# Top-k cross attention: the row maximum goes into the mask on GpSimd, and the guard's transpose, copy and transfer go

## The reference

```
q = (h @ w_q + b_q).reshape(B, L, H, D)
kv = (ctx @ w_kv + b_kv).reshape(B, Lc, 2, H, D)
k, v = (kv[:, :, 0], kv[:, :, 1])
scores = jnp.einsum('bqhd,bkhd->bhqk', q, k) / jnp.sqrt(jnp.float32(D))
top_s, top_i = jax.lax.top_k(scores, TOPK)          # TOPK = 16
attn = jax.nn.softmax(top_s, axis=-1)
vg = jnp.take_along_axis(v_bh[:, :, None, :, :], top_i[..., None], axis=3)
o = jnp.einsum('bhqk,bhqkd->bqhd', attn, vg).reshape(B, L, C)
```

## Time and profile before

| | before |
| --- | --- |
| median of 3 runs | 1315.63 us |
| span of the profiled execution | 1318.7 us |
| TensorE busy | 1221.3 us, 93% |
| VectorE busy | 1162.2 us, 88% |
| ScalarE busy | 994.5 us, 75% |
| GpSimd busy | 849.7 us, 64% |
| mean granted TensorE clock | 0.963 of full |

### The profile page before, as it was taken

How to read it: one execution, slowest core, us unless ns; L and a number is a source line. 1 busy time by engine, 2 the same in 40 slices (tenths; PEclk the granted TensorE clock), 3 DMA queues, 4 the chain that set the end, 5 groups by cost and what they waited for, 6 DMA issues and landing times. The chain is left out here.

```text
span 1318.7 us, 38821 instructions
## 1 busy us (share of the span) xinstructions
PE 1221.3 (93%) x13667; PEld 860.3 (65%) x13667; DVE 1162.2 (88%) x3854; ACT 994.5 (75%) x2001; POOL 849.7 (64%) x1134
## 2 busy tenths in 40 slices
PE   6888798999999999999999999999999999989897
PEld 5665476667676766666676766676676766656564
DVE  4469899999999999998999999999999999897443
ACT  3644487879797978878797979888797878776754
POOL 1314397958686886859496877959595868666310
PEclk8768799999999999999999999999999999989999
DMA  6531111202111121202121121312030211110110
GB/s 202 139 94 32 36 39 40 66 22 69 39 50 50 29 79 34 65 19 71 30 58 43 42 66 26 82 28 66 17 85 23 74 26 34 34 26 17 34 34 17
DMA packets 111390, 67.23 MB, mean 51 GB/s; under 512 B 13837, under 2 KB 107871, under 8 KB 111199
## 3 DMA queue, kind: packets, MB, share of 16 engines
q1 hardware_dynamic: 109166, 63.71, 18.2%
q10 hardware_dynamic: 2032, 1.05, 0.3%
HBM read 22.33 MB, written 4.19 MB: 20 GB/s over the span
## 5 line engine op out<-in xcount | busy, mean ns | idle before, releaser
L1762 ACT ACTIVATE prob<-turned_score 128x1024 f32<-128x1024 f32 x320 | 325.9, 1018 | 115.5 <-PE turned_score L1434 107.4
L2021 POOL TENSOR_TENSOR pair<-full,pair 128x512 f16<-128x512 f32 x182 | 210.6, 1163 | 108.5 <-ACT pair L1727 100.3
L2027 POOL TENSOR_SCALAR far<-far 128x512 bf16<-128x512 bf16 x256 | 158.0, 617 | 110.9 <-DVE far L1937 92.3
L1923 DVE MATCH_REPLACE8 rest<-top,score 128x256 f32<-128x256 f32 x512 | 207.7, 413 | 0.0
L1937 DVE MATCH_REPLACE8 far<-best,rest 128x256 bf16<-128x256 f32 x512 | 205.3, 408 | 1.0 <-issue 1.0
L1920 DVE MAX8 top<-score 128x8 f32<-128x256 f32 x512 | 192.2, 416 | 6.8 <-PE score L1434 6.4
L1910 DVE TENSOR_REDUCE rowmax_l<-score 128x4 f32<-128x1024 f32 x121 | 147.3, 1217 | 42.0 <-PE score L1434 29.4
L1434 PE MATMUL work<-pair_n,w_m_hi 128*128 128x256 f16 x1024 | 173.5, 274 | 1.4 <-ACT pair_n L1727 1.3
L1434 PE MATMUL work<-pair_n,w_m_lo 128*128 128x256 f16 x512 | 139.8, 273 | 0.0
L1727 ACT ACTIVATE pair<-full 128x512 f16<-128x512 f32 x192 | 121.0, 630 | 18.7 <-DMA q_stack_l<-pair 1.0
L1434 PEld LDWEIGHTS work<-pair_n,w_m_hi 128*128 128x128 f16 x1024 | 96.1, 98 | 22.3 <-issue 9.9
(11 more groups left out here) (206 smaller groups left out, 3190.9 us busy)
## 6 DMA issues: line engine op xcount, KB each, us to landing
k_stack_t<-pair SPq DMA_DIRECT2D x96, 64.0 KB, 2.3
k_stack_l<-pair SPq DMA_DIRECT2D x96, 64.0 KB, 2.3
k_stack_w<-pair SPq DMA_DIRECT2D x93, 64.0 KB, 2.3
q_stack_w<-pair SPq DMA_DIRECT2D x93, 64.0 KB, 2.3
q_stack_t<-pair SPq DMA_DIRECT2D x93, 64.0 KB, 2.3
q_stack_l<-pair SPq DMA_DIRECT2D x93, 64.0 KB, 2.3
ctx_t<-in_ctx_turned SPq DMA_DIRECT2D x16, 256.0 KB, 2.8
ctx_l<-in_ctx SPq DMA_DIRECT2D x16, 256.0 KB, 2.9
```

The costliest lines, as they stand in the source:

```text
L1762: act.activation(prob[:, at:at + 2, :], both_b[:, :, :], ACT.Exp).then_inc(exp_done, 1)
L1923: m = dve.match_replace(rest[p % 2][:, t, :], eight[:, t, :], bank[:, t * L:(t + 1) * L], -FAR)
L2021: pool.tensor_tensor(pr[:, 1, :, :], whole[:, :, :], pr[:, 0, :, :], ALU.subtract).then_inc(split_lo, 1)
L2027: pool.tensor_scalar(tile, tile, FAR, -1.0, ALU.add, ALU.mult).then_inc(far_fixed, 1)
```

## The change

The row maximum of the top-k attention no longer goes through `gd`, `gc` and `gg`. `fx` adds it on GpSimd while it makes the mask: a kept place becomes the maximum, every other one 2^100. TensorE then takes the tile off the turned scores, with an identity of -1 in place of +1. Since the maximum differs from block to block, `fx` has two operations of 128x256, each with the maximum as a scalar by partition, where it had one of 128x512 with constants alone. `b_t` has 48 rows instead of 49 and no longer waits for `guard_in`. There are three `top8` buffers in place of two, and `t1` waits for the `fx` of nine units earlier, not for a transpose. The 64 `gd_t` no longer take one of the three `work` banks.

Besides, the lists of pieces stand in the code as text (`ORDERS`), without the `gd_t`, `gc_t` and `gg_t`; all other pieces stand in the order that they had, on all five engines. `IDLE_WORK` is empty. The loads of weights are counted by their place in SP's list; their order is the old one.

```
@@ tables
-IDLE_WORK = ("a_w:0:3=12 o_w:0:1=19 bk_w:0:0=18 x4_n2:0:0=26 wp:0:17=13 a_w:1:0=7 a_t:0:0=22 a_w:1:3=14 "
...
-             "pr_l:15:0=35")
+IDLE_WORK = ("")
...
+    NTOP = 3
-        ident16 = sb("ident16", [P, P], BF16)
+        minus_ident = sb("minus_ident", [P, P], BF16)
-        top8 = [sb(f"top8_{i}", [P, 2, 2, LT, 8], F32) for i in range(2)]
+        top8 = [sb(f"top8_{i}", [P, 2, 2, LT, 8], F32) for i in range(NTOP)]
@@ tensor, gd
-                    if s == "t":
-                        src = top8[n % 2][:, :, :, :, 0].rearrange("p z h t -> p (z h t)")
-                    else:
-                        src = rowmax[s][n % 2][:, :]
-                    turn(d_take(piece, b, i)[0:8, 0:P], src).then_inc(d_ready, 1)
+                    turn(d_take(piece, b, i)[0:8, 0:P], rowmax[s][n % 2][:, :]).then_inc(d_ready, 1)
@@ tensor, b
-                    pe.wait_ge(guard_in[s], 16 * (NG * b + (i if s == "w" else i // 2) + 1))
+                    if s != "t":
+                        pe.wait_ge(guard_in[s], 16 * (NG * b + (i if s == "w" else i // 2) + 1))
...
+                        u = 16 * b + 2 * i
+                        for t in range(LT):
+                            for z in range(2):
+                                zr = slice(64 * z, 64 * z + NR)
+                                mm(bank_b[z][:, t * L:(t + 1) * L], k[zr, i, t * P:(t + 1) * P], q[zr, i, :], t == 0, False)
+                        for z in range(2):
+                            pe.wait_ge(far_fixed, u + z + 1)
                             for t in range(LT):
                                 for j in range(LT):
...
+                                    last[z] = mm(bank_b[z][:, at:at + P], far[(u + z) % NFAR][:, j, t * P:(t + 1) * P],
+                                                 minus_ident[:, :], False, (t, j) == (LT - 1, LT - 1))
@@ vector, t1
-                    if n >= 2 and i % 4 == 0:
-                        dve.wait_ge(d_ready, d_no["gd_t", (n - 2) // NG, (n - 2) % NG])
+                    if n >= NTOP and i % 4 == 0:
+                        dve.wait_ge(far_fixed, 4 * (n - NTOP) + 4)
@@ gpsimd, fx
-                    tile = far[p % NFAR][:, :, :]
-                    pool.tensor_scalar(tile, tile, FAR, -1.0, ALU.add, ALU.mult).then_inc(far_fixed, 1)
+                    for t in range(LT):
+                        half = far[p % NFAR][:, t, :]
+                        m = pool.tensor_scalar(half, half, FAR, top8[(NG * b + i // 4) % NTOP][:, z, row % 2, t, 0:1],
+                                               ALU.add, ALU.add)
+                    m.then_inc(far_fixed, 1)
```

More of the change, by code:

```diff
@@ L154, in stage_rows @@
-def stage_rows(table):
-    rows = []
-    for engine, text in table:
-        for one in text.split():
-            name, _, tick = one.partition("@")
-            stage, _, item = name.partition(":")
-            rows.append((float(tick), engine, stage, int(item)))
-    return rows
-def window_rows():
-    return stage_rows(WINDOW)
-def top_rows():
-    return stage_rows(TOP)
-def middle_rows():
-    return stage_rows(MIDDLE)
-def last_rows():
-    return stage_rows(LAST)
-def weight_rows(chunks):
-    return stage_rows(WEIGHTS)
@@ L998, in idle_work, with orders @@
     return found
-def orders(B, chunks):
-    window_at, top_at, middle_at, last_at = starts(B)
-    rows, moved = [], shifts()
-    for k, row in enumerate(weight_rows(chunks)):
-        rows.append((row[0] + WEIGHTS_AT, k, 0, row))
-    for at, group in ((window_at, window_rows()), (top_at, top_rows()), (middle_at, middle_rows()),
-                      (last_at, last_rows())):
-        for b in range(B):
-            for k, row in enumerate(group):
-                rows.append((row[0] + at[b] + moved.get((row[2], b, row[3]), 0.0), k, b, row))
-    rows.sort(key=lambda e: (e[0], e[2], e[1]))
-    return {e: [(row[2], b, row[3]) for _, _, b, row in rows if engine_of(row, b) == e]
-            for e in ("sp", "pe", "act", "dve", "pool")}
+def orders():
+    found = {}
+    for engine, text in ORDERS.items():
+        found[engine] = []
+        for one in text.split():
+            stage, b, item = (one + ":0").split(":")[:3]
+            found[engine].append((stage, int(b), int(item)))
+    return found
 def weight_chunks(C, HID):
@@ L1140, in build, with loads_in_slot @@
         chunks = weight_chunks(C, HID)
-        slot_of = [k if k < NSTAGE else (k - NSTAGE) % NLATE for k in range(len(chunks))]
         mod_src = {"ada": (ada, "L0_xcond_w_ada"), "sskv": (sskv, "L1_xcond_Wss_kv"), "ssq": (ssq, "L1_xcond_Wss_q")}
-        plan = orders(B, chunks)
+        plan = orders()
+        loads = [k[2] for k in plan["sp"] if k[0] == "wd"]
+        load_no = {k: j for j, k in enumerate(loads)}
+        slots = [j if j < NSTAGE else (j - NSTAGE) % NLATE for j in range(len(loads))]
+        slot_of = {k: slots[j] for k, j in load_no.items()}
+        def loads_in_slot(k):
+            return slots[:load_no[k] + 1].count(slot_of[k])
         def number(engine, *kinds):
@@ L1756, in _ @@
                     if n <= NPROB // 2:
-                        act.wait_ge(lo_done, max(wl_no["wl", 0, k] for k in range(NLATE, NSTAGE)))
+                        act.wait_ge(lo_done, max(wl_no["wl", 0, k] for k in loads[NLATE:NSTAGE]))
                     if n > NPROB // 2:
@@ L1848, in _ @@
                     if what == "wt":
-                        dve.wait_ge(hi_done, 1 + sum(c[0] == "wt" for c in chunks[:i]))
+                        dve.wait_ge(hi_done, wh_no["wh", 0, i])
                         dve.tensor_tensor(W[name]["lo"][:, :, n0:n0 + n], chunk_view(i), W[name]["hi"][:, :, n0:n0 + n],
```

161 lines of the change are left out of this document (27 added, 134 removed), and 1138 rows, old and new, of tables (ORDERS, SHIFTS).

## The result

| | before | after |
| --- | --- | --- |
| median (4 runs each, same chip) | 1315.2 us | 1659.3 us |
| ratio | 1 | 1.2613, 95% interval 1.2572 to 1.2654 |
| span of the profiled execution | 1318.7 us | 1656.4 us |
| GpSimd busy | 849.7 us, 64% | 1279.7 us, 77% |
| TensorE busy | 1221.3 us, 93% | 1295.4 us, 78% |

The sign was right and the size wrong: 333 us above the forecast of 1326, and far outside the range. The page after, with the lines that answer to the earlier trace rows: span, granted clock, the chain that ended last by engine.

The account below looks back on a forecast made before the run. TensorE was taken to bound the steady part, VectorE close behind, GpSimd with idle time. 1318.7 - 10 + 13 + 7 = 1328.7 us of span, a median of 1326 us, range 1307 to 1346.

Parts of the forecast that it names:

- part 2: GpSimd's fx gets longer: 0.20 to 0.50 us more a tile, 0.35 taken; loss of 13 us, bounds 0 and 34.
- Rival B: GpSimd becomes the pace: one scalar costs as much as two, +34 in place of +13; median 1347 us, chance 13%.
- part 2's own working: Extra time of 12 and 6 tiles, less waits and 1.44 us slack, before the last projection: mean 1.3 us a sample.
- the average of 75% is no free room: GpSimd's idle share of a quarter in the steady part is not free everywhere, as TensorE depends on it each sample.
- the slack ahead of the last projection: GpSimd's split for the last projection ends 1.44 us before TensorE uses it; delay beyond that makes TensorE stand.
- its 13 samples: Steady part from 200 to 1150 us, 73.2 us a sample; 1.0 us lost in each gives part 2's 13 us.
- 73.6 to 74: Sign for part 2: us for a sample between two last projections; below 73 would show Rival A.
- The estimate of 85 ns: GpSimd's cost of reading one scalar, from 102 cycles at 1.2 GHz; fx would be longer by 0.37 us.
- Part 1: Guard's 64 transposes on TensorE, with copies and transfers, go: gain of 10 us, bounds -16 and 0.
- 16 us less: Sign for Part 1: ScalarE's busy time falls by this, as 64 copies at 254 ns go.
- Part 3: Unread matmuls at start and end go: 4 us lateness given back, 11 us lost to TensorE's clock; +7, bounds -10 and +26.
- 0.62 and 0.88: Estimated TensorE clocks without unread matmuls, from 0.75 at 34 to 160 us and 0.98 at 1200 to 1312 us.

Follow-up runs that it names:

- b_two: One form run with GpSimd alone, not a whole kernel: a 128x256 add and mult operation with two scalars by partition; 552 ns.
- gapless, with guard: Kernel before with fx as two 128x256 add, mult operations, scalar by partition (512) first, constant -1.0 second, replaced places -512; 1330.2 us, ratio 1.0092.
- add-mult, changed, complete: Changed kernel with fx adding the maximum by add, then mult by 1.0, replaced places -512, exponential with a bias of -512; 1328.4 us, ratio 1.0060.
- halves, with guard: Kernel before with fx as two 128x256 add, mult operations with constants alone; 1332.4 us, ratio 1.0091.
- slow, with guard: Kernel before with fx as two 128x256 add, mult operations, constant 2^100 first, scalar by partition (-1) second; 1366.7 us, ratio 1.0358.
- add-add constants, changed: Changed kernel with fx as one 128x512 add, add operation with two constants, row maximum left out; 1550.6 us, ratio 1.1758.
- constants' version: Changed kernel with fx as one 128x512 add, mult operation with two constants, row maximum left out; 1313.9 us, ratio 0.9967.

## Why the prediction was wrong

**The failed step is part 2's bound.** "So two new operations take between 0.82 and 1.12 us": its prices by column came from rows whose operators are add and mult (the old `far` operation by its line, `normed` by its 559 ns, which `b_two` gives alone with 552). The 205 ns in the lower end are of an operation with mult and add, but of two columns, where a price by column cannot show. The new operation has add and add, which no row of before had, and I widened the bound for the scalar only. It takes 1.146 us for each half, 2.29 us a tile: +1.68 where I had +0.35 and at most +0.50. Rival B was nearest in mechanism and had the wrong size for the same reason.

With the right price, part 2's own working would have given ((12 x 1.68 - 0.6 - 1.44) + (6 x 1.68 - 0.24 - 1.44)) / 2 = 13.3 us a sample, 172 us in 13, half of the 344 us measured. So its way from tiles to time fell short too; where is shown below.

**The second error, in what counts.** I added durations. GpSimd's time for a tile is durations and the gaps at their ends. With the medians from the traces, 70 of 256 tiles following another tile: before 617 + 0.27 x 79 + 0.73 x (85 + 80) = 758 ns. The same working gives:

| kernel | tile, durations | with gaps | over before | ratio |
| --- | --- | --- | --- | --- |
| gapless, with guard | 0.96 us | 0.89 us | +0.13 | 1.0092 |
| add-mult, changed, complete | 0.95 | 0.89 | +0.13 | 1.0060 |
| halves, with guard | 0.81 | 1.00 | +0.25 | 1.0091 |
| slow, with guard | 0.96 | 1.19 | +0.43 | 1.0358 |
| add-add constants, changed | 1.93 | 2.07 | +1.31 | 1.1758 |
| the changed kernel | 2.29 | 2.52 | +1.76 | 1.2613 |

The ratios go with the last but one column (flat up to +0.25) and not with the durations: 0.96 us stands beside 1.0092 and beside 1.0358. The changed kernels have no guard, which lowers their ratio by its 7 to 9 us. From the last but one to the last it is 108.7 us for 0.45 us a tile, 0.94 of 256 x 0.45: there GpSimd is the pace, and every ns counts for each tile. Up to +0.25 a tile costs about 12 us in all, so the room is small and uneven.

**From tiles to time.** That the average of 75% is no free room was right, and so was the slack ahead of the last projection, for the steady part and for small delays. The starts of the first product of the last projection cut each profile into a start (up to that of the first sample), eleven samples and an end (from that of the twelfth). The two cuts of the kernel before, and then those of the slow `fx`:

```profile
339.76 0.38 PE L1434 MATMUL work<-w_Wp_hi,pair 128*128 128x256 f16 x2
...
1139.60 0.38 PE L1434 MATMUL work<-w_Wp_hi,pair 128*128 128x256 f16 x2
```
```profile
354.31 0.38 PE L1435 MATMUL work<-w_Wp_hi,pair 128*128 128x256 f16 x2 [0.31 <-issue]
...
1178.33 0.38 PE L1435 MATMUL work<-w_Wp_hi,pair 128*128 128x256 f16 x2
```

The same for the others, as us over before, from one profile each:

| kernel | tile over before | start | a sample | a sample by part 2's working | end |
| --- | --- | --- | --- | --- | --- |
| gapless, with guard | +0.13 | +4.0 | -0.1 | 0 | +2.0 |
| halves, with guard | +0.25 | +5.5 | +0.7 | 0.5 | +3.1 |
| slow, with guard | +0.43 | +14.6 | +2.2 | 2.0 | +6.4 |
| the changed kernel | +1.76 | +78.5 | +20.9 | 14.0 | +28.8 |

Up to +0.43 the working is right within 0.2 us a sample. What it left out is what lies before and behind its 13 samples, which I had put at nothing for part 2 without a reason. The start in the table holds two of the 13; with 13 samples taken off at the table's rates, 16 of the slow kernel's 45 us are left and 65 of the changed kernel's 338. At +1.76 it is too low in the samples as well, since TensorE then waits in more places than the one.

**The right number for the wrong reasons.** For the operation that I had priced (477 ns, I said 485) the cost over the constants' version is 0.9% or 12 us, and the forecast had 13. That is luck. Its tiles took +0.13 us and not +0.35, because the gaps went; and in the profiles a sample takes 72.3 us against 72.1 with constants and 72.7 before, where I had said 73.6 to 74, so that of the 11.4 us between the two spans only 2.5 lie in the eleven samples, 2.5 in the start and 6.4 in the end. (The exponential with a bias, 1109 ns against 1023 without, is in this kernel and not in the constants' version; it adds 11 us to ScalarE, and the run without `fx` has it at 1.0017.)

**The price of a scalar.** A scalar by partition adds 71 to 79 ns here. The estimate of 85 ns from the Trainium skill (GPSIMD Engine Reference, Performance pitfalls for Q7 kernels) is near it. The miss lay in the operators and not in the scalar.

**Part 1, -10 us.** The guard's removal was 7 us without `fx` (1.0017 to 0.9965) and 9 us with operations of the same length on both sides (1.0092 to 1.0026): right. One sign of it failed: ScalarE is busy 994.5 us before and after, not 16 us less. The 64 copies are gone, while the larger groups of its other operations each take 1 to 8 ns longer (in the constants' version it is 986.6 us); the cause stays open.

**Part 3, +7 us.** Taken out of the kernel before alone, the unread matmuls leave the clocks at 0.70 and 0.93: the signs were right, the falls about half of what I had drawn on a line through three points (0.62 and 0.88). The loss was 1 us on average and at most 4.5. The 0.64 of the changed kernel's start has its slower `fx` in it as well.

**Rival A** would have needed add and mult with constants, which is the second kernel of the experiments at 0.9967: the forecast's sum without part 2 is right within 0.2%. So nearly the whole error lies in part 2: in the price of one instruction, and in the way from its delay to time.

## What to carry to other kernels

A price holds for the operation with its operators, not for its engine and shape: where an edit brings a pair of operators that no row shows, neither end of the bound may come from another pair, and the form is worth a run by itself before the whole is priced. Where an engine's list is dense, count from start to start in the timeline rather than by the mean duration. A delay that is priced in the steady part has to be priced in the start and the end too; in the slow kernel they held some 16 of 45 us. Where a maximum is only to be added, try add and then mult by 1.0: in place of two additions it made the complete kernel 331 us shorter here, together with the loss of the constant 2^100; the second operator alone, with constants, was 237 us.

## What the hardware showed unexpectedly

- GpSimd, tensor_scalar of 128x256, by operators: add and mult 403, 475, 552 ns (none, one, two scalars by partition), add and add 1067, 1142, 1217, add alone with one scalar 924. One of 128x128 with add and add and one scalar is 715, so add and add costs 3.3 ns a column where add and mult costs 0.85.
- A constant of 2^100 or 2^20 in an operation of add and mult lengthens the time from its start to the next one's by about 100 ns (four operations of 403 ns in 1.81 us, not 1.51); the profile counts it as no one's busy time. In this kernel it was worth 35 us.
- Without `fx`, GpSimd has 158 us less to do and the time is the same (1.0017).
